# Down products two blocks behind gate and up, one state product a block later, and a new order of the first products

## The reference

```
x = x + LN(attn(LN(x)))
x = x + LN(ffn(LN(x)))

attn(h): h = h + mamba2(rmsnorm(h) * ln1_w)
         u = rmsnorm(h) * ln2_w
         return h + (silu(u @ gate_w.T) * (u @ up_w.T)) @ down_w.T     # 512 -> 1792 -> 512
mamba2:  in-projection 512 -> 1284, causal convolution of 4 taps and silu,
         chunked state space scan (2 chunks of 128 tokens, 4 heads), times silu(z), out-projection
ffn(t):  t @ W_up.T + the rank-8 correction of the one expert of 4 that a gate picks for the token
```

## Time and profile before

| | us |
|---|---|
| median of the runs (3; 780.35 to 781.87) | 780.83 |
| the profiled execution | 783.21 |
| its span, first to last instruction | 781.5 |
| TensorE busy in it | 746.2 (95%) |
| VectorE busy | 513.3 (66%) |
| ScalarE busy | 342.5 (44%) |
| GpSimd busy | 149.6 (19%) |
| matmuls gate and up / down | 312.1 / 163.4 |

### The profile page before, as it was taken

How to read it: one execution, slowest core, us unless ns; L and a number is a source line. 1 busy time by engine, 2 the same in 40 slices (tenths; PEclk the granted TensorE clock), 3 DMA queues, 4 the chain that set the end, 5 groups by cost and what they waited for, 6 DMA issues and landing times.

```text
span 781.5 us, 14105 instructions
## 1 busy us (share of the span) xinstructions
PE 746.2 (95%) x5626; PEld 533.6 (68%) x5634; DVE 513.3 (66%) x1181; ACT 342.5 (44%) x615; POOL 149.6 (19%) x201
## 2 busy tenths in 40 slices
PE   4999979989999999999999999999999999999985
PEld 3767846668666877588666877578666876667752
DVE  6798877787665757477664767467674767365356
ACT  2653766545623374235623363235633264222221
POOL 2220131105100321104200231103300241001021
PEclk8899999999999999999999999999999999999997
DMA  8970000030203120040202211050201201031001
GB/s 308 386 237 5 2 27 1 1 82 2 55 1 55 55 50 6 1 109 1 55 1 51 60 30 25 1 108 3 55 1 32 77 1 29 1 81 29 28 1 54
DMA packets 60082, 41.12 MB, mean 53 GB/s; under 512 B 45680, under 2 KB 45808, under 8 KB 60016
## 3 DMA queue, kind: packets, MB, share of 16 engines
q1 hardware_dynamic: 60016, 40.22, 18.6%
HBM read 25.01 MB, written 4.19 MB: 37 GB/s over the span
## 4 chain that ended last, share of the span: by engine, by line
PE 84%; DVE 8%; ACT 3%; DMA 2%; issue 1%; SPq 1%; POOL 0%; ACTq 0%; DVEq 0%
PE gu L1447 35%; PE wa L1447 24%; PE acc L1447 18%; PE wc L1447 6%; DVE xbc L1051 2%; DMA weights<-in_w_up 2%; DVE weights L973 2%; ACT weights L617 1%; DVE sg L1189 1%; DVE stats_a L1245 0%; DMA h2t<-xbc 0%; SPq L364 0%; DVE xbc L1177 0%; DVE hn L1251 0%; ACT sg L751 0%
## 5 line engine op out<-in xcount | busy, mean ns | idle before, releaser
L1447 PE MATMUL gu<-h2t,weights 128*128 128x256 f16 x2688 | 312.1, 273 | 1.9 <-DVE h2t L1183 1.0
L1447 PEld LDWEIGHTS gu<-h2t,weights 128*128 128x128 f16 x2688 | 261.9, 98 | 52.1 <-issue 10.3
L1447 PE MATMUL acc<-weights,act 128*128 128x512 f16 x672 | 163.4, 379 | 4.9 <-DVE act L1194 4.9
L1189 DVE SCALAR_TENSOR_TENSOR sg<-gu,bound,sg 128x256 f32<-128x256 f32 x112 | 53.2, 475 | 102.2 <-ACT sg L751 101.4
L751 ACT ACTIVATE sg<-gu,scale_inv 128x256 f32<-128x256 f32 x112 | 53.0, 473 | 146.5 <-PE gu L1447 146.3
L1447 PE MATMUL wa<-ht,weights 128*128 128x256 f16 x912 | 107.3, 275 | 1.3 <-DMA ht<-ra 1.1
L1447 PEld LDWEIGHTS acc<-weights,act 128*128 128x128 f16 x672 | 65.2, 98 | 62.2 <-DVE act L1194 6.9
L1447 PEld LDWEIGHTS wa<-ht,weights 128*128 128x128 f16 x912 | 90.0, 99 | 19.1 <-DMA ht<-ra 1.6
L761 ACT ACTIVATE act<-sg 128x256 f16<-128x256 f32 x112 | 46.6, 416 | 101.0 <-DVE sg L1189 101.0
L1194 DVE TENSOR_TENSOR act<-sg,act 128x256 f16<-128x256 f32 x112 | 49.8, 445 | 54.0 <-ACT act L761 54.0
L1051 DVE SCALAR_TENSOR_TENSOR xbc<-wa,conv_ws,xbc 128x253 f32<-128x253 f32 (+1 forms) x132 | 57.3, 476 | 1.8 <-ACT xbc L664 0.2
(11 more groups left out here) (233 smaller groups left out, 872.6 us busy)
## 6 DMA issues: line engine op xcount, KB each, us to landing
xa<-in_x SPq DMA_DIRECT2D x9, 512.0 KB, 3.6
weights<-in_x SPq DMA_DIRECT2D x7, 512.0 KB, 3.9
out_x<-h SPq DMA_DIRECT2D x14, 256.0 KB, 2.2
weights<-in_w_in SPq DMA_DIRECT2D x5, 512.0 KB, 6.5
weights<-in_w_down SPq DMA_DIRECT2D x3, 768.0 KB, 13.2
weights<-in_w_gate SPq DMA_DIRECT2D x2, 1024.0 KB, 13.6
weights<-in_w_up SPq DMA_DIRECT2D x2, 1024.0 KB, 14.0
weights<-in_w_gate SPq DMA_DIRECT2D x2, 768.0 KB, 14.4
```

What stands on the lines that cost most here:

```text
L1189: nc.vector.scalar_tensor_tensor(sg[:, f % 2], GU[f % 2][:, SEQ:2 * SEQ], up_to_act, sg[:, f % 2], ALU.mult, ALU.mult).then_inc(sem("prod_ ...
L1447: return nc.tensor.matmul(dst, left, right, start=start, stop=stop)
```

## The change

Three orders on TensorE's queue are changed; no instruction is added or removed, and no other engine's program changes.

1. The down product of block f - 2, not f - 1, follows gate and up of block f (`BEHIND = 2`). Blocks 0 and 1 then have none, and down products 12 and 13 stand at the end of the step, behind `a_in(g + 1, 0)`.
2. In step 1 (g == 1) `a_state` moves from the end of block 6 to block 7, behind gate and up 7 and down 5 and ahead of `a_y(1, 0)`.
3. In the prologue `a_in(0, 0)` goes ahead of the squares of the first up piece, behind those of the first gate piece.

```diff
--- before.py
+++ after.py
@@ -1723,8 +1723,8 @@
 
             A_AT = {0: lambda g: g > 1 and a_in(g, 1), 1: lambda g: (a_in(g, 2), a_dt(g)), 2: lambda g: a_z(g, 0),
                     3: lambda g: a_z(g, 1), 4: lambda g: (a_tok(g), a_dec(g, 0), a_dec(g, 1)),
-                    5: lambda g: (a_att(g, 0), a_dec(g, 2)), 6: lambda g: (a_att(g, 1), a_state(g)),
-                    7: lambda g: (a_y(g, 0), a_y(g, 1)), 8: lambda g: a_y_spread(g), 9: lambda g: a_o(g, 0),
+                    5: lambda g: (a_att(g, 0), a_dec(g, 2)), 6: lambda g: (a_att(g, 1), g > 1 and a_state(g)),
+                    7: lambda g: (g == 1 and a_state(g), a_y(g, 0), a_y(g, 1)), 8: lambda g: a_y_spread(g), 9: lambda g: a_o(g, 0),
                     10: lambda g: a_o(g, 1)}
             NEXT_AT = {13: lambda g: a_in(g, 0)}
             C_AT = {6: lambda g: c_logits(g), 7: lambda g: c_zt(g),
@@ -1740,8 +1740,8 @@
                         pe.wait_ge(sem("lora_split"), 2)
                     if b is not None:
                         b_gu(b, f)
-                        if f:
-                            b_down(b, f - 1)
+                        if f >= BEHIND:
+                            b_down(b, f - BEHIND)
                     if a is not None and f in A_AT:
                         A_AT[f](a)
                     if c is not None and f in C_AT:
@@ -1749,7 +1749,8 @@
                     if a is not None and a + 1 < GROUPS and f in NEXT_AT:
                         NEXT_AT[f](a + 1)
                 if b is not None:
-                    b_down(b, FBLK - 1)
+                    for f in range(FBLK - BEHIND, FBLK):
+                        b_down(b, f)
 
             def grams(*ns):
                 for n in ns:
@@ -1761,8 +1762,9 @@
                 a_t1(0)
                 grams(*IN[3:])
                 spread(0)
-                grams(GATE[0], UP[0])
+                grams(GATE[0])
                 a_in(0, 0)
+                grams(UP[0])
                 a_dt(0)
                 a_in(0, 1)
                 a_in(0, 2)
@@ -1797,6 +1799,8 @@
 
 
 RING = 4
+
+BEHIND = 2
 
 
 def slot(f):
```

## The result

The changed kernel took 780.42 us (median of 14 runs, 778.64 to 781.62), the kernel before, in 14 runs beside it, 781.70 us (779.72 to 783.96). The ratio is 0.9975 [0.9965, 0.9985], so 1.95 us less (1.2 to 2.7). One execution of `e14_dt_first_all` (802.86 us) and one of `e15_dt_first_two_waits` (1086.8) ran slow at a lower clock and are in no ratio. The forecast was 3.3 us less. The direction was right, the size was not, and 780.42 lies just above the range. Of the 2.9 us between it and 777.5, 0.9 is the base (the three runs shown before had a median of 780.83, fourteen have 781.70).

What follows compares the result with a forecast made beforehand. TensorE, busy throughout the middle steps, was taken as the bound. Gains of 2.0 (prologue), 1.3 and 0.9 (steps 7, 8) less 0.9 (step 1) made 3.3 us: from 780.83 to 777.5 us, range 775.9 to 779.1.

Steps and rivals of the forecast that it cites:

- Edit 3, 2.0 us: Prologue: `a_in(0, 0)` ahead of the first up squares gains 2.0 us, bounds 0.7 and 3.9.
- the start of `a_in(0, 0)` at 19.2: Prologue: split weights are there when the squares of gate end, so `a_in(0, 0)` starts at 19.2, without a wait.
- The 5.5 us of unbroken work: Prologue: the clock rises 5.5 us after unbroken work begins at 17.51, so at 23.0 instead of about 25.7.
- Edits 1 and 2, steps 2 to 6: Middle steps: TensorE's lead of 1.3 us meets no late operand; 0 gained, bounds 0 and 0.5 us lost a step.
- The rival that was slower: Middle steps: the lead meets a late operand at `a_o(g, 0)`, bringing the clock down, up to 790.7 us; chance 0.05.
- Steps 7 and 8: Waits ahead of down product 13 go, covered by the down products before it: 1.3 and 0.9 us gained.
- the lag buys nothing: Rival: the last group's transposed input, or VectorE in the tail, sets steps 7 and 8: 779.7 us; chance 0.1.
- (c): End of step 1: the clock falls behind the joined wait for `ht`; 1.5 us lost, bounds 0 and 2.7.
- (b): End of step 1: two waits join into one of 3.2 us for `ht`; step 2 starts 0.2 us later.
- (a): Step 1: the state product's 2.46 us wait goes, shorter waits precede the outputs; 0.8 us gained, bounds 0 and 1.6.
- the tail, put at 0: Serial tail after step 8: no change in its own length, with some 0.9 us either way left open.
- the early rise doesn't come: Rival, prologue: the clock rises at 25.7 as before, so the reorder gives only 0.7 us: 778.8 us; chance 0.15.

Runs made afterwards that it cites:

- e14_dt_first_all: Changed kernel with `a_dt` also ahead of the squares of the first up piece: 780.44 us, ratio 0.9964 to the kernel before.
- e15_dt_first_two_waits: Changed kernel with down product 12 of step 1 ahead of `a_in(2, 0)` and `a_dt` ahead of the first up squares: 778.86 us, 0.9953.
- e1: Kernel before with only `a_in(0, 0)` moved ahead of the squares of the first up piece: 782.62 us, 0.9996.
- e5: Kernel before with the second gate piece loaded ahead of the first up piece, so the up piece lands later: 784.45 us, 1.0043.
- e8: Kernel before with the last `w_in` piece loaded behind the first gate piece, and `a_in(0, 0)` ahead of the first up squares: 784.03 us, 1.0042.
- e10: Changed kernel with down product 12 of step 1 ahead of `a_in(2, 0)`, parting the wait for `ht` in two: 778.49 us, 0.9955.
- e3: Kernel before with only the state product of step 1 moved to block 7: 781.43 us, 0.9984.
- e13: Kernel before with only the prologue reordered: `a_in(0, 0)` and `a_dt` both ahead of the squares of the first up piece: 780.69 us, 0.9989.
- e9: Changed kernel with the old prologue order, and down product 12 of step 1 ahead of `a_in(2, 0)`: 779.89 us, 0.9961.
- e4: Kernel before with down products two blocks behind and the state product of step 1 moved, prologue order unchanged: 778.87 us, 0.9970.
- e2: Kernel before with only the down products two blocks behind: 780.28 us, 0.9972.
- e7: Kernel before with the last `w_in` piece loaded behind the first gate piece, so it lands later: 781.99 us, 1.0005.
- e6: Kernel before with the second gate piece loaded ahead of the first up piece, and `a_in(0, 0)` ahead of the first up squares: 781.34 us, 0.9989.
- e12: The changed kernel unchanged, profiled once more: 780.59 us.

## Why the prediction was right or wrong

**Edit 3, 2.0 us: wrong, and the step that failed is its first,** the start of `a_in(0, 0)` at 19.2. "They are there when the squares of gate end" rests on the split at 18.84 of the earlier trace rows, and so on one execution, in which the split came 0.95 us earlier than in any other of the table. The four profiles of the table with edit 3 have the first split at 18.4 to 20.4, and `a_in` 0.9 us later. The order took the wait for the up piece away (0.81 in the earlier trace rows) and put one for the split in its place, up to 2.37 us. In place of the 2.0 us the runs show a term of 0.3 us (e1; between 1.5 less and 0.8 more), with a sign that the landing sets (e5 to e8). The prediction looked only at what `a_in` had to wait for in the trace, not at what the squares of up had been covering. Two smaller steps went with it. The 5.5 us of unbroken work, by which the clock was to rise at 23.0, begins with the squares of gate only if nothing stands behind them; in the changed kernel the wait does, and the rise is at 26.3. Nor is 5.5 us a constant of this kernel, as the next paragraph shows. And the squares of up between `a_in` and `a_dt` stand on the path of VectorE, at some 0.9 us (e15). The sum had them there too, so that is no error of it, but part of why nothing is left once the premise falls. Where the premise holds, the start does too: e10 has 19.28 for 19.2, and its prologue is 2.95 us shorter than that of before, between the forecast 2.0 and its bound 3.9. That is one profile, helped by a rise of the clock at 21.3 for the forecast 23.0; beside e3, the old order with the clock held (70.97), it gains 1.06. That the whole 2 us would pass through to step 1 was right: from L1065 to the first gate product it is 45.69 us before, 45.37 after, 45.34 in e13.

The Trainium skill ("TensorE: Matmul & The Clock Gate", What's actually happening) let the rise of the clock move by about 0.5 us from run to run. The runs show more: with the old order, counted from the start of the squares of up, the rise came after 4.4 us in e9, 5.5 in the profile before and 5.9 in e4 (means of the clock in the 1 us window of the rise: 0.54, 0.64, 0.62). And in e3 the clock held ahead of `a_in`, which cost 2.62 us there and 4.68 in e4.

**Edits 1 and 2, steps 2 to 6: right.** 88.88 us a step before and after; the lead of 1.3 us met no late operand. The rival that was slower did not come.

**Steps 7 and 8: right,** 1.31 and 0.87 us, and so the rival "the lag buys nothing" falls. Down product 13 of both steps runs without a wait in every kernel with edit 1.

**Step 1: the parts right, one of them mis-sized.** (c), the half clock behind the joined wait, was priced at 1.5 and measured 4.15 - 2.62 = 1.53; it came in four of the five profiles with that wait, and not in e2. (b), 0.2, was measured as the 0.16 us between step 1 of e2 and of before (92.99 and 92.83), though both hold a fall of the clock. (a) was taken at 0.8, halfway between a clock that holds in the two waits ahead of the outputs and one that doesn't. It held, so (a) is the term that was mis-sized: from the first gate product of step 1 to gate and up 8 it is 52.70 us where it was 54.19, 1.49 us gained. The waits, 2.14 and 0.31 us, are near those forecast (2.4 and 0.5).

The prediction knew that step 1 of the trace before holds a fall, behind the wait for the state; what it did not see is that not every execution has it. Of nine profiles in which the state product stands in block 6, five (before among them) show it at half clock behind its wait of 2.5 us, a sixth (e7) shows the fall one product later (gate and up 7 cost 4.29 us there), and three (e6, e8, e13) show full clock behind the same 2.46 us. These three took 91.5 us for step 1, as e3 did; the six took 92.8 to 93.0. All seven profiles with edits 1 and 2 have 92.5 to 93.2 us, each with one stretch of half clock: behind the wait for `ht` (after, e4, e12, e14) or at the outputs (e9, e10, e15). So beside a kernel whose clock holds the edits cost 1.0 to 1.7 us in step 1, and beside one whose clock falls between 0.5 less and 0.5 more.

**The sum.** With the term of edit 3 at nothing the forecast would have been 1.3 us less than before, within the measured 1.2 to 2.7. That is in part luck: with (a) at its measured size it is 2.0, and the tail, put at 0, gave another 0.7. The tail took 26.5 to 26.8 us in the five profiles with edit 1 and the joined wait, and 27.2 to 28.0 in the other twelve; why it goes with them was not looked into. The timed runs give edits 1 and 2 2.3 us (e4, 0.7 to 4.0), and the profiles with edit 1 show 1.9 to 2.2 of it in steps 7 and 8. The rival "the early rise doesn't come" named about the right price for edit 3 (0.7 where e1 measured 0.3, with 0.7 inside its interval), for a reason that isn't the cause: the start of `a_in`, not only the clock, was late.

**What stays open.** Why `w_in` lands 2.4 us earlier in one execution than in another was not found. In the two profiles compared here, the transfers moved less in the first microseconds of the late one. The kernel before (last two columns: share of the DMA engines, GB/s):

```profile
5.00:6.00 1.00, 0.00 (x0) 0.00 (x0) 0.97 (x3) 0.00 (x0) 0.00 (x0) 1.00 1.02 375
```

and the changed one:

```profile
5.00:6.00 1.00, 0.00 (x0) 0.00 (x0) 0.97 (x4) 0.00 (x0) 0.00 (x0) 1.00 0.57 131
```

What makes that dip is not shown. Nor is it shown why the clock falls behind one wait and holds behind another of the same length.

## What to carry to other kernels

A product that looks as if it only waited may be the cover of another's landing: before it is moved back, ask how late the operand of what takes its place can be, over several profiles, since the start of this kernel differs by 2 us from one to the next. A lag between producer and consumer pays at the ends of the pipeline, where a chain has no other work beside it (here 2.2 us of steps 7 and 8), and nothing in steps that TensorE already fills. A wait behind which the trace shows half clock is a term with two values, and its removal is worth the smaller of them until several profiles say otherwise.

## What the runs showed of the hardware

- **Landing of the first transfers.** With the same order of loads TensorE's first squares of `w_in` started between 6.95 and 9.35 us from the start; the first split of weights moved with them, 17.43 to 20.39.
- **The clock behind one and the same wait.** After 2.46 us without work in block 6 of step 1 (2.59 in e2), the state product took 2.04 us in five profiles and 1.10 us in three, and 1.14 in e7, with the fall behind it; after 3.1 us for `ht`, `a_in` took 2.6 us in one and 4.2 to 4.3 in four. A stretch of half clock in step 1 costs 1.2 to 1.5 us (92.8 to 93.0 against 91.5).
- **The rise of the clock.** In the nine prologues of the table in which the clock had fallen, it was back between 3.7 us (e10) and 5.9 us (e4) after the start of the unbroken work ahead of the rise.
- **The same program, another place.** Up to the outputs of step 1, e9 is the same program as e4, and e10 as the changed kernel. The outputs ran at half clock in e9 and e10 and at full clock in e4 and the changed kernel, behind the same waits (2.14 and 0.2 to 0.3 us). e15 and e14 are such a pair too, behind the same 2.14 us.
